# TensorE's first stage as two loops, and two edge-table compares on GpSimd, in a graph-attention layer

## The chip, the cores and the metric

The kernel runs on one core of one Trainium2 chip. The metric is the device time of one execution in microseconds; the kernel before took 474.52 us (median of 3 runs, 474.12 to 474.85). TensorE does the matmuls, VectorE (DVE) and ScalarE (ACT) read PSUM and split numbers, GpSimd (POOL) issues scattered transfers and does small arithmetic, SyncE (SP) issues most transfers.

## The reference

One layer over 384 nodes of 1024 features, in float32:

```
xn = layernorm(x)                                        # 384 x 1024
q, k, v = xn @ wq.T + bq, xn @ wk.T + bk, xn @ wv.T + bv
q2, k2, v2 = heads(q @ wiq.T + biq), heads(k @ wik.T + bik), heads(v @ wiv.T + biv)   # 16 heads of 64
mask = full((384, 384), -inf); mask[src, dst] = softplus(w)[type - 1]   # 12288 edges; diagonal: w[3] where empty
attn = softmax(q2 @ k2^T / 8 + mask)
gnn  = (attn @ v2) @ wo.T + bo
mq, mk = exp(-(xn @ Wq + bq)^2 / 2), exp(-(xn @ Wk + bk)^2 / 2)
mix  = (sum_per_head(mq * mk) * (xn @ Wv + bv)) @ Wo + bo
x    = x + gnn + mix
h    = layernorm(x)      # then the expert with the smallest loss is chosen for all of h
out  = x + h @ base_W.T + base_b + (relu(h @ down_W[e] + down_b[e]) @ up_W[e] + up_b[e]) @ conv_W[e].T + conv_b[e]
```

## The kernel before

Every float32 matrix product is made of three products of a shorter format: each operand is split into a high part (rounded by ScalarE, w_hi or T_hi) and a low part (the rest, by VectorE, w_lo or T_lo), and TensorE adds hi x hi, lo x hi and hi x lo into one PSUM bank.

The engines' programs are written out by hand, one instruction stream for each, and nothing but semaphores ties them together. Weights come as blocks of 128x1024 (512 KB) in rotating slots: SyncE loads a block into raw, ScalarE makes w_hi (line 536), VectorE w_lo (line 895), TensorE uses both and frees them.

The first stage has 32 jobs, 8 for each of q, k, v and q2. A job (column_job, lines 1272 to 1284) waits for the slot's high part (hi_ready), issues 16 matmuls of 128x384 (line 1278), waits for the low part (lo_ready), issues 8 more (line 1283) and frees the slot (w_used). Ahead of it TensorE waits until the PSUM bank is free (bank_free). Jobs go round four slots and four banks, so job a has slot and bank a % 4 and use number a // 4. Slot 3 of the four lies in the memory of other tiles, so its blocks are called mask, probT_hi and probT_lo in the profile. Jobs 0 and 1 are written out apart; jobs 2 to 31 come from one Python loop, which leaves 30 x 24 matmuls one behind the other in TensorE's program. Jobs 2 to 23 multiply xT, jobs 24 to 31 T0.

Beside it, the edge mask is built. GpSimd scatters the 12288 edge values into four tables in device memory (96 indirect transfers, line 454), since an edge may occur twice and the last one counts; then it loads them back (line 463): table 0 into mask, tables 1 to 3 into the tile U. VectorE fills the diagonal (lines 975 and 979) and merges tables 1 to 3 into mask, one after another (merge_table): a compare with the blank value -1e30 writes present (line 986), and a predicated copy takes what is present (line 988). present is one place in U, so each compare waits for the copy before it. Behind the merge come the eight head pairs: scores (line 1404), softmax (maximum at 1060, exponential on ScalarE at 659, reciprocal at 1069), turning by a transfer through device memory, and the product with V (line 1416). GpSimd's next work behind the table loads is a cast of V (line 485).

Of the kernel before, what the change touches and what calls it, by code (L numbers as in the profile page):

```python
# [18 lines left out]
U32 = mybir.dt.uint32  # L19
ALU = mybir.AluOpType  # L20
# [5 lines left out]
N = 384  # L26
D = 1024
NT = N // P
KB = D // P
# [3 lines left out]
CH = E // P  # L33
CJ = 3
STEPS = CH // CJ
STREAMS = 4
# [7 lines left out]
ABSENT = -1e30  # L44
# [5 lines left out]
FIRST = 32  # L50
# [4 lines left out]
A_SLOTS = (0, 1, 2, SLOTS + SPARE - 1)  # L55
A_USES = [(A_SLOTS[a % 4], a // 4) for a in range(FIRST)]
A_BANKS = (0, 1, 6, 7)
# [43 lines left out]
def gps_layer(nc, x, out, weights, conv, down, upT, up_b, down_b, conv_b, disc, bias_cols,  # L101
              rows, edge_weights, edge_rows, edge_cols, consts):
    with ExitStack() as ctx:
        def sb(name, shape, dt):
            return ctx.enter_context(nc.sbuf_tensor(name, shape, dt))

        def sem(name):
            return ctx.enter_context(nc.semaphore(name))
# [10 lines left out]
        xT = [sb(f"xT_{c}", [P, KB, N], F32R) for c in ("hi", "lo")]  # L119
        T0 = [sb(f"T0_{c}", [P, KB, N], F32R) for c in ("hi", "lo")]  # L120
# [6 lines left out]
        U = sb("U", [P, 6 * D], F32)  # L127
# [2 lines left out]
        key_row = U[:, 3456:3456 + 2 * CJ * P].rearrange("p (s n) -> p s n", s=2)  # L130
        key_junk = U[:, 4224:4352]
        later = [U[:, g * NT * N:(g + 1) * NT * N].rearrange("p (t n) -> p t n", t=NT) for g in range(STREAMS - 1)]
        present = U[:, 4608:4608 + NT * N].rearrange("p (t n) -> p t n", t=NT)
        prob = U[:, 0:2 * NT * N].rearrange("p (h t n) -> p h t n", h=2, t=NT)
        sq_q = U[:, 2304:2688]
        sq_k = U[:, 2688:3072]
# [105 lines left out]
        bank_free = [sem(f"bank_free{s}") for s in range(len(A_BANKS))]  # L242
        dup_ready = sem("dup_ready")
# [3 lines left out]
        diag_step = sem("diag_step")  # L247
        scattered = [sem(f"scattered{g}") for g in range(STREAMS)]
        table_in = [sem(f"table_in{g}") for g in range(1, STREAMS)]
        mask_step = sem("mask_step")  # L250
        v_copied = sem("v_copied")
        v_tile = sem("v_tile")
        vh_ready = sem("vh_ready")
# [169 lines left out]
        def _(pool):  # L423
# [25 lines left out]
            for k in range(CH):  # L449

                g = QUARTERS[k % STREAMS]
# [6 lines left out]
            for g, into in enumerate([mask[:]] + later):  # L458
                pool.wait_ge(scattered[g], 16 * (DEEP + 1))
                if g == 0:  # L460

                    pool.wait_ge(lo_ready[A_SLOTS[3]], FIRST // 4 + 1)
                pool.dma_start(into, tables[g].rearrange("(t p n) o -> p t (n o)", t=NT, p=P)).then_inc(
                    table_in[g - 1] if g else first_mask_in, 16)

            def mix_lo(j):

                pool.wait_ge(mh_ready, j + 1)
                pool.tensor_tensor(T2[1][:, j, :], mix_v, T2[0][:, j, :].bitcast(F32),  # L469
                                   ALU.subtract).then_inc(ml_ready, 1)  # L470
# [339 lines left out]
        def _(dve):  # L810
# [36 lines left out]
            def turned(t, which=0):  # L847
                b = LN_BANKS[which][t]
                return PS[:, b:b + 2, :].rearrange("p b (k n) -> p (b k) n", k=4), slice(t * P, (t + 1) * P)
# [48 lines left out]
            for t in range(NT):  # L898
                dve.wait_ge(xt_hi, t + 1)
                src, r = turned(t)  # L900
# [81 lines left out]

            def merge_table(g):

                dve.wait_ge(table_in[g], 16)
                dve.tensor_scalar(present, later[g], ABSENT, None, ALU.not_equal).then_inc(mask_step, 1)
                dve.wait_ge(mask_step, 2 * g + 1)
                dve.copy_predicated(mask[:].rearrange("p t n -> p (t n)"),
                                    present.bitcast(U32).rearrange("p t n -> p (t n)"),
                                    later[g].rearrange("p t n -> p (t n)")).then_inc(mask_step, 1)  # L990
                dve.wait_ge(mask_step, 2 * g + 2)

            for a in range(FIRST):
                job(a)
# [33 lines left out]
            for g in range(STREAMS - 1):  # L1028
                merge_table(g)
# [232 lines left out]
        def _(pe):  # L1262
# [9 lines left out]
            def column_job(slot, use, src, bank):  # L1272

                o = PS[:, bank, 0:N]
                pe.wait_ge(hi_ready[slot], use + 1)
                for part in range(2):
                    for k in range(KB):
                        pe.matmul(o, w_hi[slot][:, k * P:(k + 1) * P], src[part][:, k, :],  # L1278
                                  start=(k == 0 and part == 0), stop=False)
                pe.wait_ge(lo_ready[slot], use + 2)  # L1280
                for k in range(KB):
                    wl = w_lo[slot][:, k * P:(k + 1) * P]
                    last = pe.matmul(o, wl, src[0][:, k, :], start=False, stop=(k == KB - 1))  # L1283
                last.then_inc(w_used[slot], 1)
# [58 lines left out]
            def whole_part(a, wide, part, start, stop):  # L1343

                for k in range(KB):
                    last = pe.matmul(PS[:, A_BANKS[a], 0:N], wide[A_SLOTS[a]][:, k * P:(k + 1) * P],  # L1346
                                     xT[part][:, k, :], start=(start and k == 0), stop=(stop and k == KB - 1))
                return last
# [16 lines left out]
            whole_part(1, w_hi, 1, False, False)  # L1365
            pe.wait_ge(lo_ready[A_SLOTS[1]], 2)
            whole_part(1, w_lo, 0, False, True).then_inc(w_used[A_SLOTS[1]], 1)
            for a in range(2, FIRST):
                pe.wait_ge(bank_free[a % 4], a // 4 + 1)
                column_job(*A_USES[a], T0 if a >= 3 * KB else xT, A_BANKS[a % 4])  # L1370

            for half in range(2):
                for kp in range(4):
# [238 lines left out]
```

## Time and profile before

| | us |
|---|---|
| median of 3 runs (lowest, highest) | 474.52 (474.12, 474.85) |
| the profiled execution's own time | 474.66 |
| its span, first to last instruction | 472.9 |
| TensorE busy | 465.9 |
| VectorE, ScalarE, GpSimd busy | 342.3, 262.2, 157.2 |

The span is what the profile's rows cover; its own time is 1.8 us longer. TensorE's matmuls are pipelined: one 128x384 matmul is shown with 0.33 us, but the next begins 0.17 us behind it. So a dense stretch is read from the distance of the starts, not from the durations.

### The profile page before, as it was taken

The numbers are of one execution on the slowest core, as the hardware profiler recorded it, in microseconds if no ns is written. First come the engines' busy times: TensorE is split into PE (matmuls) and PEld (weight loads), VectorE is DVE, ScalarE is ACT, GpSimd is POOL, SyncE is SP. The second block draws the span as 40 slices with busy tenths as digits, with TensorE's granted clock in tenths as the row PEclk, the third lists the DMA queues.
The fourth block names the chain that finished last, engine by engine and source line by source line (L and its number), as shares of the span: only waits on it lengthen the run. The fifth ranks groups of instructions, "written<-read, shape, count | busy, mean of one in ns | idle before, by whom it ended". The sixth has DMA issues, their size and how long they took to land.

```text
span 472.9 us, 7361 instructions
## 1 busy us (share of the span) xinstructions
PE 465.9 (99%) x2533; PEld 432.4 (91%) x2533; DVE 342.3 (72%) x796; ACT 262.2 (55%) x429; POOL 157.2 (33%) x176
## 2 busy tenths in 40 slices
PE   7999999999999999999999999999999999999996
PEld 5999999999999888999999999999998888888885
DVE  6979966677626259687978888796966794587294
ACT  3734433333324245788989889897974542163170
POOL 3147677777767741002130202212142000050200
PEclk9999999999999999999999999999999999999999
DMA  8877756655444454577675766766679835210463
GB/s 243 325 230 230 239 195 167 176 182 180 154 152 153 133 200 179 175 226 253 205 232 184 235 192 197 247 180 224 192 240 382 308 115 179 89 46 0 155 247 133
DMA packets 39049, 91.92 MB, mean 194 GB/s; under 512 B 7410, under 2 KB 20306, under 8 KB 38884
## 3 DMA queue, kind: packets, MB, share of 16 engines
q1 hardware_dynamic: 33604, 83.15, 54.0%
q0 software_dynamic: 4832, 7.45, 4.7%
q10 hardware_dynamic: 576, 0.85, 0.5%
q8 instruction: 20, 0.33, 0.3%
q14 instruction: 17, 0.14, 0.1%
HBM read 77.96 MB, written 13.47 MB: 193 GB/s over the span
## 4 chain that ended last, share of the span: by engine, by line
PE 87%; DVE 5%; DMA 3%; ACT 3%; issue 1%; SPq 0%; DVEq 0%; ACTq 0%
PE PS L1278 32%; PE PS L1288 28%; PE PS L1283 16%; PE PS L1416 3%; PE PS L1404 2%; DMA turn<-U 2%; PE PS L1535 2%; PE PS L1346 2%; DMA U<-x 1%; DVE U L1076 1%; DVE w_lo L895 1%; PE PS L1266 1%; ACT U L659 1%; PE PS L1539 1%; ACT w_hi L536 1%
## 5 line engine op out<-in xcount | busy, mean ns | idle before, releaser
L895 DVE TENSOR_TENSOR w_lo<-raw,w_hi 128x1024 fp32r<-128x1024 f32 x86 | 104.4, 1225 | 45.0 <-ACT w_hi L536 45.0
L536 ACT ACTIVATE w_hi<-raw 128x1024 fp32r<-128x1024 f32 x87 | 90.8, 1054 | 68.5 <-PE PS L1288 44.1
L454 POOL DMA_INDIRECT table<-evalue,where x96 | 103.0, 1073 | 45.7 <-issue 25.2
L1283 PE MATMUL PS<-xT_hi,w_lo 128*128 128x384 f32 x320 | 61.9, 334 | 0.0
L1278 PE MATMUL PS<-xT_hi,w_hi 128*128 128x384 f32 x320 | 61.9, 334 | 0.0
L1278 PE MATMUL PS<-xT_lo,w_hi 128*128 128x384 f32 x320 | 61.9, 334 | 0.0
L1278 PEld LDWEIGHTS PS<-xT_lo,w_hi 128*128 128x128 f32 x320 | 56.0, 188 | 0.0
L1278 PEld LDWEIGHTS PS<-xT_hi,w_hi 128*128 128x128 f32 x320 | 56.0, 188 | 0.0
L1283 PEld LDWEIGHTS PS<-xT_hi,w_lo 128*128 128x128 f32 x320 | 56.0, 188 | 0.0
L469 POOL TENSOR_TENSOR T_lo<-U,T_hi 128x384 fp32r<-128x384 f32 x8 | 8.2, 1020 | 97.8 <-ACT T_hi L733 97.8
L1288 PE MATMUL PS<-w_hi,T_hi 128*128 128x512 f32 x144 | 40.0, 391 | 0.0
L1288 PE MATMUL PS<-w_hi,T_lo 128*128 128x512 f32 x144 | 39.8, 389 | 0.0
L950 DVE SCALAR_TENSOR_TENSOR U<-U,V,cst 128x128 f32<-128x128 f32 x96 | 33.6, 350 | 6.0 <-DMA U<-key_dram 3.7
L1288 PE MATMUL PS<-w_lo,T_hi 128*128 128x512 f32 x144 | 37.8, 389 | 0.0
L598 ACT ACTIVATE T_hi<-PS,bias 128x384 fp32r<-128x384 f32 x24 | 13.8, 576 | 41.7 <-PE PS L1283 41.7
L1288 PEld LDWEIGHTS PS<-w_hi,T_lo 128*128 128x128 f32 x144 | 27.0, 188 | 5.7
L1288 PEld LDWEIGHTS PS<-w_lo,T_hi 128*128 128x128 f32 x144 | 27.0, 188 | 5.6
L1288 PEld LDWEIGHTS PS<-w_hi,T_hi 128*128 128x128 f32 x144 | 27.0, 188 | 5.2
L1076 DVE STREAM_TRANSPOSE U<-U 128x384 f32<-128x384 f32 x48 | 24.0, 551 | 10.5 <-DMA turn<-U 10.5
L659 ACT ACTIVATE U<-U,nmax 128x384 f32<-128x384 f32 x48 | 28.9, 605 | 3.7 <-DVE nmax L1064 3.7
L965 DVE SCALAR_TENSOR_TENSOR T_lo<-PS,bias,T_hi 128x384 fp32r<-128x384 f32 x24 | 14.8, 615 | 16.1 <-ACT T_hi L598 16.1
L666 ACT ACTIVATE U<-U,rsum 128x384 f32<-128x384 f32 x48 | 25.8, 604 | 0.0
(241 smaller groups left out, 817.1 us busy)
## 6 DMA issues: line engine op xcount, KB each, us to landing
raw<-weights SPq DMA_DIRECT2D x84, 512.0 KB, 4.6
turn<-U SPq DMA_DIRECT2D x16, 576.0 KB, 4.0
U<-turn SPq DMA_DIRECT2D x64, 144.0 KB, 2.9
U<-key_dram SPq DMA_DIRECT2D x32, 192.0 KB, 4.1
mask<-weights SPq DMA_DIRECT2D x9, 512.0 KB, 5.1
table<-Q POOLq DMA_DIRECT2D x4, 576.0 KB, 9.5
V<-conv SPq DMA_DIRECT2D x4, 512.0 KB, 5.4
U<-table POOLq DMA_DIRECT2D x3, 576.0 KB, 7.5
```

Of the source, the lines that this page charges most:

```text
L454: pool.indirect_dma_start(tables[g], bass.IndirectOffsetOnAxis(ap=where[:, k:k + 1], axis=0), evalue[:, k:k + 1], None, bounds_check=N * N ...
L536: act.activation(w_hi[slot][:], raw[slot][:], ACT.Copy).then_inc(hi_ready[slot], 1)
L659: act.activation(prob[:, h, t, :], prob[:, h, t, :], ACT.Exp, bias=nmax[:, h, t:t + 1], scale=SCALE, accum_out=ssum[:, h, t:t + 1]).then_i ...
L666: act.activation(prob[:, h, t, :], prob[:, h, t, :], ACT.Copy, scale=rsum[:, h, t:t + 1]).then_inc(prob_ready, 1)
L895: dve.tensor_tensor(w_lo[slot][:], raw[slot][:], w_hi[slot][:].bitcast(F32), ALU.subtract).then_inc(lo_ready[slot], 1)
L950: dve.scalar_tensor_tensor(out=key_junk, in0=key_row[:, s, c * P:(c + 1) * P], scalar=ekey[:, ch0 + c:ch0 + c + 1], in1=tri, op0=ALU.is_eq ...
L965: dve.scalar_tensor_tensor(out=dst[1][:, j, :], in0=PS[:, A_BANKS[a % 4], 0:N], scalar=bias[:, a:a + 1], in1=dst[0][:, j, :].bitcast(F32), ...
L1076: dve.transpose(blocks.rearrange("p (c m t i) -> p t m c i", c=NQ, m=NT, t=NT)[:, t], prob[:, h, t, :].rearrange("p (m c i) -> p m c i", m ...
L1278: pe.matmul(o, w_hi[slot][:, k * P:(k + 1) * P], src[part][:, k, :], start=(k == 0 and part == 0), stop=False)
L1283: last = pe.matmul(o, wl, src[0][:, k, :], start=False, stop=(k == KB - 1))
L1288: return pe.matmul(bank, src[part][:, 2 * kp + k2, t * P:(t + 1) * P], weights_in[slot][:, k2 * HALF:(k2 + 1) * HALF], start=start, stop=stop)
L1416: last = pe.matmul(PS[:, 7, 0:N], vs[:, m, h, :], probT[part][:, m, :], start=(m == 0 and part == 0), stop=(m == NT - 1 and part == 1))
```

## The change

TensorE: jobs 2 and 3 stay written out. Jobs 4 to 31 become two loops that run on TensorE alone, each pass four jobs (one for each slot and bank): five passes over xT, two over T0. The numbers that the jobs wait for come from the loop's register. GpSimd: behind its four table loads it compares tables 1 and 2 with the blank value (is_gt instead of not_equal) and raises found. present has two places now, the first where the key rows of the duplicate search were, the second where it was; so the first compare waits for that search (dup_ready) and the second for the diagonal (diag_step). VectorE keeps the compare of table 3 and the three copies.

```diff
--- before.py
+++ after.py
@@ -130,7 +130,7 @@
         key_row = U[:, 3456:3456 + 2 * CJ * P].rearrange("p (s n) -> p s n", s=2)
         key_junk = U[:, 4224:4352]
         later = [U[:, g * NT * N:(g + 1) * NT * N].rearrange("p (t n) -> p t n", t=NT) for g in range(STREAMS - 1)]
-        present = U[:, 4608:4608 + NT * N].rearrange("p (t n) -> p t n", t=NT)
+        present = [U[:, c:c + NT * N].rearrange("p (t n) -> p t n", t=NT) for c in (3456, 4608)]
         prob = U[:, 0:2 * NT * N].rearrange("p (h t n) -> p h t n", h=2, t=NT)
         sq_q = U[:, 2304:2688]
         sq_k = U[:, 2688:3072]
@@ -248,6 +248,7 @@
         scattered = [sem(f"scattered{g}") for g in range(STREAMS)]
         table_in = [sem(f"table_in{g}") for g in range(1, STREAMS)]
         mask_step = sem("mask_step")
+        found = sem("found")
         v_copied = sem("v_copied")
         v_tile = sem("v_tile")
         vh_ready = sem("vh_ready")
@@ -463,6 +464,15 @@
                 pool.dma_start(into, tables[g].rearrange("(t p n) o -> p t (n o)", t=NT, p=P)).then_inc(
                     table_in[g - 1] if g else first_mask_in, 16)
 
+            for g in range(STREAMS - 2):
+
+                pool.wait_ge(table_in[g], 16)
+                if g == 0:
+                    pool.wait_ge(dup_ready, CH)
+                if g == 1:
+                    pool.wait_ge(diag_step, 2 * NT)
+                pool.tensor_scalar(present[g], later[g], ABSENT, None, ALU.is_gt).then_inc(found, 1)
+
             def mix_lo(j):
 
                 pool.wait_ge(mh_ready, j + 1)
@@ -982,13 +992,16 @@
 
             def merge_table(g):
 
-                dve.wait_ge(table_in[g], 16)
-                dve.tensor_scalar(present, later[g], ABSENT, None, ALU.not_equal).then_inc(mask_step, 1)
-                dve.wait_ge(mask_step, 2 * g + 1)
+                if g < STREAMS - 2:
+                    dve.wait_ge(found, g + 1)
+                else:
+                    dve.wait_ge(table_in[g], 16)
+                    dve.tensor_scalar(present[0], later[g], ABSENT, None, ALU.not_equal).then_inc(found, 1)
+                    dve.wait_ge(found, g + 1)
                 dve.copy_predicated(mask[:].rearrange("p t n -> p (t n)"),
-                                    present.bitcast(U32).rearrange("p t n -> p (t n)"),
+                                    present[g % 2].bitcast(U32).rearrange("p t n -> p (t n)"),
                                     later[g].rearrange("p t n -> p (t n)")).then_inc(mask_step, 1)
-                dve.wait_ge(mask_step, 2 * g + 2)
+                dve.wait_ge(mask_step, g + 1)
 
             for a in range(FIRST):
                 job(a)
@@ -1365,9 +1378,15 @@
             whole_part(1, w_hi, 1, False, False)
             pe.wait_ge(lo_ready[A_SLOTS[1]], 2)
             whole_part(1, w_lo, 0, False, True).then_inc(w_used[A_SLOTS[1]], 1)
-            for a in range(2, FIRST):
-                pe.wait_ge(bank_free[a % 4], a // 4 + 1)
-                column_job(*A_USES[a], T0 if a >= 3 * KB else xT, A_BANKS[a % 4])
+            for a in (2, 3):
+                pe.wait_ge(bank_free[a], 1)
+                column_job(*A_USES[a], xT, A_BANKS[a])
+
+            for src, begin, end in ((xT, 1, 3 * KB // 4), (T0, 3 * KB // 4, FIRST // 4)):
+                with pe.Fori(0, end - begin) as i:
+                    for s in range(4):
+                        pe.wait_ge(bank_free[s], i + (begin + 1))
+                        column_job(A_SLOTS[s], i + begin, src, A_BANKS[s])
 
             for half in range(2):
                 for kp in range(4):
```

TensorE's program around the start of job 4, before (names as in the profile; x8 is eight alike):

```order
L1278 MATMUL PS<-xT_lo,probT_hi 128x384 x8
L1283 MATMUL PS<-xT_hi,probT_lo 128x384 [waits lo_ready6]
L1283 MATMUL PS<-xT_hi,probT_lo 128x384 x7
L1278 MATMUL PS<-xT_hi,w_hi 128x384 [waits hi_ready0,bank_free0]
L1278 MATMUL PS<-xT_hi,w_hi 128x384 x7
L1278 MATMUL PS<-xT_lo,w_hi 128x384 x8
```

And now, at the same place (column_job's lines are 1291 to 1296 there, the loops' line is 1386):

```order
L1291 MATMUL PS<-xT_lo,probT_hi 128x384 x8
L1296 MATMUL PS<-xT_hi,probT_lo 128x384 [waits lo_ready6]
L1296 MATMUL PS<-xT_hi,probT_lo 128x384 x7
L1386 UNCONDITIONAL_BRANCH
L1386 ISA
L1291 MATMUL PS<-xT_hi,w_hi 128x384 [waits hi_ready0,bank_free0]
L1291 MATMUL PS<-xT_hi,w_hi 128x384 x7
L1291 MATMUL PS<-xT_lo,w_hi 128x384 x8
L1293 REGISTER_ALU
```

Up to the branch TensorE issues 21 + 8 + 4 + 16 + 104 = 153 matmuls and transposes in both. The end of a pass, which before was simply the next job:

```order
L1296 MATMUL PS<-xT_hi,probT_lo 128x384 x7
L1386 REGISTER_ALU
L1386 COMPARE_AND_BRANCH
L1386 UNCONDITIONAL_BRANCH
L1386 ISA
L1291 MATMUL PS<-T_hi,w_hi 128x384 [waits hi_ready0,bank_free0]
```

The last four rows are the way into the second loop; the branch back goes to the first ISA row. VectorE's program at the merge, before:

```order
L986 TENSOR_SCALAR U<-U 128x1152 [waits table_in1]
L988 COPY_PREDICATED mask<-U 128x1152 [waits mask_step]
L986 TENSOR_SCALAR U<-U 128x1152 [waits table_in2,mask_step]
L988 COPY_PREDICATED mask<-U 128x1152 [waits mask_step]
L986 TENSOR_SCALAR U<-U 128x1152 [waits table_in3,mask_step]
L988 COPY_PREDICATED mask<-U 128x1152 [waits mask_step]
```

and now:

```order
L1001 COPY_PREDICATED mask<-U 128x1152 [waits found]
L1001 COPY_PREDICATED mask<-U 128x1152 [waits found,mask_step]
L999 TENSOR_SCALAR U<-U 128x1152 [waits table_in3,mask_step]
L1001 COPY_PREDICATED mask<-U 128x1152 [waits found]
```

Two of three compares have left VectorE. GpSimd has them, now:

```order
L464 DMA U<-table 128x3x384 [waits scattered3]
L474 ISA
L474 TENSOR_SCALAR U<-U 128x1152 [waits dup_ready,table_in1]
L474 TENSOR_SCALAR U<-U 128x1152 [waits diag_step,table_in2]
L495 CAST vs<-V 128x6x64 [waits v_copied]
```

The two compares stand between the last table load and the cast of V, which before followed each other. The ISA row stood behind the cast before.

## Rows read from the trace of the kernel before

**Rows 1.** The page: span, busy time, TensorE's granted clock, the chain that ended last.

```profile
span 472.9 us, 7361 instructions
PE 465.9 (99%) x2533; PEld 432.4 (91%) x2533; DVE 342.3 (72%) x796; ACT 262.2 (55%) x429; POOL 157.2 (33%) x176
...
PEclk9999999999999999999999999999999999999999
...
PE 87%; DVE 5%; DMA 3%; ACT 3%; issue 1%; SPq 0%; DVEq 0%; ACTq 0%
```

**Rows 2.** The waits of TensorE: us in total, times, longest.

```profile
PE PS L1416 <- DVE probT_lo L1041: 0.2, 1, 0.2
```

**Rows 3.** In order of time, 29 to 50 us: start us, us, engine, line.

```profile
29.80 1.34 PEld L1283 LDWEIGHTS PS<-xT_hi,probT_lo 128*128 128x128 f32 x8 [0.26 <-DVE probT_lo L895]
31.30 1.55 PE L1278 MATMUL PS<-xT_hi,w_hi 128*128 128x384 f32 x8
31.45 1.22 DVE L895 TENSOR_TENSOR w_lo<-raw,w_hi 128x1024 fp32r<-128x1024 f32 x1
47.94 1.55 PE L1278 MATMUL PS<-xT_hi,w_hi 128*128 128x384 f32 x8
```

**Rows 4.** In order of time, VectorE, 177 to 190 us.

```profile
177.95 1.23 DVE L895 TENSOR_TENSOR w_lo<-raw,w_hi 128x1024 fp32r<-128x1024 f32 x1 [0.83 <-ACT w_hi L536]
179.09 0.75 DVE L986 TENSOR_SCALAR U<-U 128x1152 f32<-128x1152 f32 x1
...
184.64 1.55 DVE L988 COPY_PREDICATED mask<-U 128x1152 f32<-128x1152 uint32 x1
...
187.80 0.17 DVE L1064 TENSOR_SCALAR nmax<-smax 128x3 f32<-128x3 f32 x1
...
189.54 2.35 DVE L895 TENSOR_TENSOR w_lo<-raw,w_hi 128x1024 fp32r<-128x1024 f32 x2
```

**Rows 5.** The chain of waits, 189 to 206 us: start us, us, what.

```profile
189.10 3.72 ACT U L659 x12
...
192.84 0.18 DVE rsum L1069
...
205.95 1.33 PE PS L1416 x6
```

**Rows 6.** In order of time, TensorE, the first scores, 184 to 187 us.

```profile
184.78 0.45 PE L1404 MATMUL PS<-T_hi,q_hi 64*128 64x384 f32 x2
...
186.56 1.66 PE L1278 MATMUL PS<-T_hi,w_hi 128*128 128x384 f32 x8
```

**Rows 7.** The page, DMA queues: packets, MB, share of 16 engines.

```profile
q8 instruction: 20, 0.33, 0.3%
```

**Rows 8.** The same queue in 41.5 to 42.5 us.

```profile
q8 instruction: 1, 0.02, 5.5%
```

**Rows 9.** TensorE by stretch: us, busy (matmuls), clock, DMA share, GB/s.

```profile
0.00:42.00 42.00, 39.09 (x215) 1.00 0.81 263
```

**Rows 10.** DMA issues: times, KB each, median us to landing.

```profile
U<-down_b SPq DMA_DIRECT2D x1, 0.2 KB, 2.4
```

**Rows 11.** In order of time, GpSimd, the whole span.

```profile
2.75 1.08 POOL L438 MEMSET Q<- 128x1152 f32 x1
...
185.55 0.96 POOL L485 CAST vs<-V 128x384 fp32r<-128x384 f32 x1 [11.74 <-ACT V L613]
...
220.97 0.50 POOL L485 CAST vs<-V 128x384 fp32r<-128x384 f32 x1 [2.54 <-PE PS L1416]
221.55 1.01 POOL L487 TENSOR_TENSOR vs<-V,vs 128x384 fp32r<-128x384 f32 x1
```

**Rows 12.** Line 463: its table loads into U; landing of the first and the last.

```profile
L463 POOL DMA_DIRECT2D U<-table x3: 758/774/812, 171.5 to 173.1; - x3
...
DMA to landing us min/median/max: 6.8/6.8/6.8
...
DMA to landing us min/median/max: 10.1/10.1/10.1
```

## The prediction

> **What bounds the kernel now.** I read the page's shares first: TensorE is busy 99% of a span of 472.9 us and carries 87% of the chain that ended last, at full granted clock (the 2.4 GHz level) from end to end [rows 1]. So only what makes TensorE wait, or stops it waiting, can move the end. The list of waits says how little it waits: between its start-up and its tail the one row is 0.2 us at line 1416 [rows 2]. The stretch that the loops replace is the densest of all. In the order of time each group of eight 384-column matmuls takes 1.39 us (31.30 to 47.94 is exactly twelve of them: 16.64 us, four jobs), and job 4, the first that goes into a loop, begins at 31.30 [rows 3]. Nothing can be won inside it; a loop can only cost.
>
> The edge tables matter elsewhere, on VectorE between 179 and 187 us, where three compares (0.75 us each) and three predicated copies (1.55 us each) stand ahead of the first softmax [rows 4]. The chain of waits shows what carries the program there: not VectorE's merge but ScalarE, which copies the last tile of V, splits two weight blocks, loads its table and starts the exponentials at 189.10; VectorE comes in at 192.84, and the first value product starts at 205.95 [rows 5]. That is where the 0.2 us of [rows 2] are. A microsecond added to this chain is a microsecond at the end, since TensorE is already waiting for it.
>
> **The change, part by part: the loops.** The matmuls are the same 28 x 24; what comes on top is control. One pass of a loop holds 96 matmuls, one fused register instruction, two register additions and a compare-and-branch; a plain branch leads into each loop, and the jobs' waits compare with a register. The profile before has no row for a register or branch instruction of TensorE. Two rows bound them. The 18 narrow score matmuls from 184.78 to 186.56 are 36 instructions (a weight load and a matmul each) in 1.78 us [rows 6], so TensorE's sequencer hands over an instruction in 0.05 us or less, while a wide pair is used up in 0.173 us. From below the price is nothing; from above I take 0.3 us for each, near the one stretch without work that the weight loads show in this stage, 0.26 us [rows 3].
>
> These are paid beside the matmuls as long as the sequencer is ahead of the array. How far ahead it is can be read from code loading. The instruction queue q8 brought 20 pieces, 0.33 MB, so 16 KB each [rows 7]. For 2533 matmuls that is one piece per 127, so the second border lies near matmul 250. A piece came between 41.5 and 42.5 [rows 8], but by 42.0 only 215 matmuls had started [rows 9]. If this is the second one, called for as the sequencer passes the second border, it is some 32 matmuls ahead, 32 x 0.173 = 5.5 us. Two places need a look.
> - Entry into the first loop. Job 3's low part was 0.26 us late (weight load at 29.80, released by VectorE) [rows 3], so here the lead is near nothing. The 16 instructions behind it are handed over in at most 0.8 us, by 30.6, and the next weight load is due at about 31.1. Three control instructions stand between (a branch, the register instruction, a wait), and they have 0.5 us; at 0.3 us each they would be 0.4 us late. I take 0, by the nearer row, and keep 0.4 as the end.
> - The back edges: four taken ones in the first loop, one in the second. The first pass ends with matmul 153 + 96 = 249 (153 from the order of the instructions), that is, right at the second border, so the loop's head and its tail lie in different pieces of code. If the head has to be brought again, the price is at least a small transfer's 2.4 us from issue to landing [rows 10], with 1.1 us for the piece itself (0.3% of 16 x 472.9 us, over 20) [rows 7]: about 3.5 us. The queue in front of the array holds 5.5 us. And the next job's weights are not late: VectorE's split for job 4 began at 31.45, ended at 32.7 and was used at about 34.1 [rows 3], and that margin grows, since a job takes TensorE 4.16 us and VectorE's share of it less. After a fetch of 3.5 us the sequencer is 2 us ahead and gains about 0.1 us with every matmul. I take 0 for each edge.
>
> The Trainium skill (Runtime: NRT & Kernel Launch, Instruction fetch mechanics) says that a taken branch whose target is not in the current two pages forces a fetch before execution can go on, and calls it a stall. That rule speaks against this change, and it is the first rival below; what I set against it is only the 5.5 us of queued matmuls.
>
> **The compares.** VectorE loses two compares (2 x 0.79 us with their gap) and gains two waits for GpSimd. GpSimd gains two compares of 128x1152. It has no such row: the 128x1152 memset took 1.08 us, the cast of 128x384 0.50 us (three times that is 1.5), the tensor_tensor of 128x384 1.01 us (three times 3.05) [rows 11]. A compare reads one operand like the cast, so I take 1.3 us and keep 1.08 and 3.05 as ends. The start is set by the tables: the first of the three lands at 171.5 + 6.8 = 178.3, the last at 173.1 + 10.1 = 183.2 [rows 12].
>
> Do GpSimd and VectorE work side by side there? The cast at 185.55 took 0.96 us beside a predicated copy that ran until 186.19, against 0.50 us alone [rows 4, 11]: GpSimd stood still until VectorE was done. So I add them up one after another. Compare 0 can run once the weight split of 177.95 is over, 179.1 to 180.4; then copy 0 (1.55), compare 1 (1.3), copy 1 (1.55) in either order to 184.8; then compare 2 on VectorE, 0.76, and copy 2, 1.55: 187.2 with the gaps. Before it was 186.19 [rows 4]. The merge ends 1.0 us later, not 1.6 us earlier. If copies and compares overlapped, the last table (183.2) would set it, and it would end at about 185.6. The Trainium skill (SBUF — State Buffer, SBUF: two separate sides) calls the shared port pair an exclusive lock that blocks the loser; the trace agrees for the cast.
>
> What waits for the merge: the first maximum, which before was ready 1.78 us after it at 187.97 [rows 4] and now at 189.0; ScalarE begins its exponentials at 189.10 [rows 5]. Cost nothing. Behind the maxima VectorE has two weight splits of 2.35 us together, begun at 189.54 [rows 4], now at 190.6, ending at 192.9, and the second reciprocal, which stood at 192.84 [rows 5], comes at 193.1. That is 0.2 us on the chain. GpSimd's next work, the cast for V at 185.55, is not delayed, and nobody else queues behind its two waits. If the compares cost 1.08 us and nothing blocks, the merge ends at 185.5 and the chain gains nothing, because ScalarE holds it. The other end is the second rival.
>
> Sum: loops 0, compares +0.2 us. The profiled execution took 474.66 us (span 472.9 and 1.8 around it), so 474.9; it was 0.14 above the median of the three runs, 474.52. I say 474.8.
>
> **The rivals.** (1) The back edge stalls. If the border is crossed and the sequencer first lets the piece after the border arrive and only then fetches the head, it is two transfers: 2 x 3.5 = 7 us, less the 5.5 us of queue, 1.5 us at each of four edges: +6 us, 480.7; with one slow transfer of 6.5 us, +4 us, 478.7. What speaks for it: the border lies in the last job, and the DMA engines are 81% busy in the first 42 us [rows 9]. Against it: 20 borders were crossed before without a single wait of TensorE. This is the slower one: it decides as soon as a fetch takes longer than 5.5 us.
> (2) The compares cost like a two-operand operation, 3.05 us. Then the merge ends at 179.1 + 3.05 + 1.55 + 3.05 + 1.55 + 2.35 = 190.7; the maximum comes at 192.4, the exponentials 3.3 us late, the second reciprocal some 3.7 us: 478.4. At 2.2 us for a compare the merge ends at 189.0, the maximum comes 1.7 us after 189.1, and the end is some 1.9 us later, 476.6. The point from which it costs is near 1.3 us, so it is close; for it the first use of an operation on GpSimd, against it that only one operand is read.
> (3) Faster: the two engines overlap after all, VectorE's earlier splits pull the chain, and the wait of 0.2 us at 205.95 goes [rows 2]: 474.66 - 0.2 = 474.5. More than that TensorE does not wait anywhere in reach, so this one can't be told from no change.
>
> **How the numbers follow.** Forecast 0.70, rival 1 0.13, rival 2 0.12, rival 3 0.05. A measurement of this kernel tells about 0.2% from no change, 0.95 us. Of the forecast I give 0.03 to slower and 0.07 to faster, for what no row of before shows; of rivals 1 and 2 0.02 and 0.01 are too small to see, and all of rival 3. Slower 0.03 + 0.11 + 0.11 = 0.25; faster 0.07; the same 0.60 + 0.02 + 0.01 + 0.05 = 0.68. The forecast's own range is 474.1 to 475.6. For 8 in 10 I go up into both slow cases until a tenth is left above: 473.9 to 477.8.
>
> **What would show it.** In the profile after: the eights of the first stage still 1.39 us apart with no idle before them, at the end of each pass of twelve in particular (47.9, 64.6, 81.2, 97.9), and job 31 ending near 147.8. A gap at just those times is rival 1. The number of q8 pieces: 16 or 17 if a loop keeps its code, some four to eight more if the head is fetched again. On GpSimd the two compares, 1.1 to 1.5 us each, not lying over VectorE's copies; VectorE's third copy ending at about 187; the exponentials at 189.1 after the start of the stage as before; the first value product at most 0.3 us later. Wrong I am if TensorE waits over 1 us in all between 31 and 206 us, or if its matmuls are not spaced as before within a pass.

## The result, and the profile after

The changed kernel took 482.55 us (median of 4 runs: 483.10, 482.61, 482.49, 480.51); the kernel before took 474.33 beside it. The medians lie 8.2 us apart, and the time is outside the range given. The ratio is 1.0143 (95% interval 1.0094 to 1.0191), which is 4.5 to 9.1 us: slower. Here and in the table below a ratio is estimated from the faster runs of each kernel alone (those within 1.5% of its fastest) and is not the quotient of the medians beside it. The profiled execution took 483.1 us, its span is 481.3, against 472.9. All rows here are of one kernel each; in the changed kernel the numbers of VectorE's lines are 10 to 13 higher and those of TensorE's 13 to 19 (1278 is now 1291, 1060 is 1073).

The page of the changed kernel, to be laid beside [rows 1, 7]:

```profile
span 481.3 us, 7393 instructions
PE 469.3 (98%) x2533; PEld 435.5 (90%) x2533; DVE 341.5 (71%) x794; ACT 261.5 (54%) x429; POOL 167.7 (35%) x178
...
PEclk9999999999999999799999999999999999999999
...
q8 instruction: 16, 0.26, 0.2%
...
PE 72%; DMA 11%; issue 5%; DVE 5%; POOL 4%; ACT 1%; POOLq 0%; DVEq 0%; SPq 0%; ACTq 0%
```

GpSimd's busy time grew by 10.5 us. In the chain that ended last transfers now have 11% (3% before) and GpSimd 4% (none before), and one slice of 40, from 192 to 205 us, has less than the full clock. The list of TensorE's waits shows what is new against [rows 2]:

```profile
PE PS L1291 <- DVE smax L1073: 5.2, 1, 5.2
```

**The first stage.** In order of time (start, duration, engine, line), the last part of job 3, the start of the first loop, of its second pass and of the second loop, and the first matmul behind the stage:

```profile
30.45 1.34 PEld L1296 LDWEIGHTS PS<-xT_hi,probT_lo 128*128 128x128 f32 x8 [0.88 <-DVE probT_lo L905]
...
31.95 1.55 PE L1291 MATMUL PS<-xT_hi,w_hi 128*128 128x384 f32 x8
...
48.59 1.55 PE L1291 MATMUL PS<-xT_hi,w_hi 128*128 128x384 f32 x8
...
115.15 1.55 PE L1291 MATMUL PS<-T_hi,w_hi 128*128 128x384 f32 x8
...
148.43 1.55 PE L1301 MATMUL PS<-w_hi,T_hi 128*128 128x512 f32 x6
```

From 31.95 to 48.59 are the same 16.64 us as in [rows 3], and five passes to 115.15 are 5 x 16.64. The 28 jobs in the loops take 116.48 us (31.95 to 148.43), and they took 116.48 before (31.30 to 147.78). Neither the control instructions nor the back edges cost anything. Nor was code fetched for them: the queue q8 brings one piece between 42 and 43 us and then none until 128, where the kernel before has one each near 63, 84, 105 and 126 us. So at no back edge of the first loop was the head brought again. The whole stage is 0.65 us late because job 3's low part came 0.88 us late instead of 0.26 [rows 3], ahead of the loops.

**The merge.** GpSimd and VectorE of the changed kernel, 172 to 197 us, beside [rows 4]:

```profile
172.97 0.82 POOL L464 DMA_DIRECT2D mask<-table  x1 [3.47 <-DMA table<-evalue,where]
...
179.97 8.67 POOL L474 TENSOR_SCALAR U<-U 128x1152 f32<-128x1152 f32 x2 [3.86 <-DMA U<-table]
...
189.29 2.16 POOL L497 TENSOR_TENSOR vs<-V,vs 128x384 fp32r<-128x384 f32 x1
```

```profile
179.88 1.23 DVE L905 TENSOR_TENSOR w_lo<-raw,w_hi 128x1024 fp32r<-128x1024 f32 x1
184.14 1.55 DVE L1001 COPY_PREDICATED mask<-U 128x1152 f32<-128x1152 uint32 x1 [3.03 <-POOL U L474]
188.74 1.88 DVE L1001 COPY_PREDICATED mask<-U 128x1152 f32<-128x1152 uint32 x1 [3.05 <-POOL U L474]
190.65 1.42 DVE L999 TENSOR_SCALAR U<-U 128x1152 f32<-128x1152 f32 x1
192.10 1.43 DVE L1001 COPY_PREDICATED mask<-U 128x1152 f32<-128x1152 uint32 x1
193.58 0.55 DVE L1073 CUSTOM_DVE_ANT_0 U<-PS,mask 128x384 f32<-128x384 f32 x1
...
196.68 0.08 DVE L1073 DVE_READ_ACCUMULATOR2_ANT smax<- 128x1 f32 x1
```

The chain of waits splits the 8.67 us into the two compares, and takes the way over both:

```profile
179.97 4.14 POOL U L474
184.10 0.08 issue
184.18 4.46 POOL U L474
```

Two compares that VectorE did in 0.75 us each take GpSimd 4.14 and 4.46 us. VectorE stands for 3.03 and 3.05 us, and the merge ends at 193.5 instead of 186.2: 7.3 us later. Of these, 0.9 are the later start of the first compare, which waited for its table (179.97 for 179.09), 3.4 the first compare, 2.5 the step from the first copy to the third compare (184.14 to 190.65, before 179.88 to 183.85), and 0.5 the last compare and copy, beside which GpSimd works on V. Not all of the 7.3 comes from the compares. The mask's table was late too, so VectorE's diagonal and the split behind it ended at 181.1 instead of 179.2. With its three compares still on VectorE, this merge would have ended 1.9 us later than before (an estimate from these rows), and 5.4 us are left for the move.

**TensorE.** Its waits and matmuls behind the scores, and the clock by stretch (us, busy, granted clock, DMA share, GB/s):

```profile
190.09 1.55 PE L1296 MATMUL PS<-T_hi,w_lo 128*128 128x384 f32 x8
196.82 2.93 PE L1291 MATMUL PS<-xT_hi,w_hi 128*128 128x384 f32 x8 [5.17 <-DVE smax L1073]
199.55 2.76 PE L1291 MATMUL PS<-xT_lo,w_hi 128*128 128x384 f32 x8
202.11 1.59 PE L1296 MATMUL PS<-xT_hi,w_lo 128*128 128x384 f32 x8
203.54 1.55 PE L1291 MATMUL PS<-xT_hi,w_hi 128*128 128x384 f32 x8
```

```profile
190.00:195.00 5.00, 1.65 (x10) 1.00 0.00 0
195.00:200.00 5.00, 3.18 (x10) 0.54 0.18 53
200.00:205.00 5.00, 5.00 (x25) 0.78 0.74 272
205.00:210.00 5.00, 5.00 (x31) 1.00 0.48 127
```

Here is what I had not seen. In the code of the first pair, TensorE itself waits for VectorE's sixth score read (score_read, whose count starts at 1, so the 7 waited for is six reads) between the pair's first and second column job. Before, the sixth read ended at 189.43 and the second job began at 190.82, as it was due: 1.4 us of slack. Now the job was due at 191.5 and the read ends at 196.76. Behind the wait the granted clock is 0.54 of full, near the lower level (1.2 GHz), and three groups of eight (196.82 to 203.54) take 6.72 us instead of 4.16. So 0.65 + 5.17 + 2.56 = 8.4 us, and the span is 8.4 us longer. By the starts alone, the group behind these three begins 8.55 us later (203.54 for 194.99), so the sum closes to about 0.2 us.

### The profile page after: what moved, and what is told of

It is laid out like the page before. It is cut to its first block, busy times and chain, and to the rows that moved or that the text cites. A ratio compares the mean times of both kernels' runs of the same rounds, so it can differ in the third digit from the quotient of the medians.

```text
span 481.3 us, 7393 instructions
## 1 busy us (share of the span) xinstructions
PE 469.3 (98%) x2533; PEld 435.5 (90%) x2533; DVE 341.5 (71%) x794; ACT 261.5 (54%) x429; POOL 167.7 (35%) x178
## 4 chain that ended last, share of the span: by engine, by line
PE 72%; DMA 11%; issue 5%; DVE 5%; POOL 4%; ACT 1%; POOLq 0%; DVEq 0%; SPq 0%; ACTq 0%
PE PS L1291 28%; PE PS L1301 20%; PE PS L1296 14%; DMA table<-evalue,where 5%; PE PS L1435 3%; PE PS L1423 2%; POOL table L455 2%; POOL U L474 2%; PE PS L1554 2%; DMA mask<-table 1%; DMA turn<-U 1%; DVE w_lo L905 1%; DMA raw<-weights 1%; DMA U<-x 1%; DMA key_dram<-V 1%
## 5 line engine op out<-in xcount | busy, mean ns | idle before, releaser
L1291 PE MATMUL PS<-xT_hi,w_hi 128*128 128x384 f32 x320 | 63.3, 339 | 5.2 <-DVE smax L1073 5.2
L1291 PE MATMUL PS<-xT_lo,w_hi 128*128 128x384 f32 x320 | 63.1, 339 | 0.0
L1291 PEld LDWEIGHTS PS<-xT_hi,w_hi 128*128 128x128 f32 x320 | 57.1, 191 | 5.5 <-DVE smax L1073 5.5
L1291 PEld LDWEIGHTS PS<-xT_lo,w_hi 128*128 128x128 f32 x320 | 57.2, 191 | 0.0
```

## The experiments

The kernels ran in five sessions, each with the kernel before beside them. In the first three the kernel before had medians of 497 to 500 us instead of 474, though one of its runs took 480.37. The trace of loops_2 shows a part of it: in 90 to 120 us the transfers moved 135 GB/s and TensorE was busy for 27.0 us of the 30, where the kernel before in its own profile had 173 GB/s and 30.0 us. The gaps of TensorE (10.8 us in the whole trace) are put down to nothing that the profile shows, so their cause is open. These sessions say little of small differences in time, but their traces do tell durations and waits. I draw nothing from the ratios of session 1: the 29 runs of the kernel before reach from 487 to 507 us, and the other medians lie within 0.1% of theirs but for e5_fill, although the ratios of both e1_loops and e2_compares lie above 1 by more than their intervals. The fourth and fifth were like the first measurement; I call those undisturbed and the first three disturbed.

| session; the kernel before | run | median us | ratio (95%) |
|---|---|---|---|
| 1; 497.38 | e1_loops, loops alone | 497.70 | 1.0125 (1.002, 1.0229) |
| 1 | e2_compares, compares alone | 497.80 | 1.0106 (1.0051, 1.0162) |
| 1 | e3_add | 497.81 | 1.0032 (0.9987, 1.0078) |
| 1 | e5_fill | 502.99 | 1.0129 (1.0077, 1.018) |
| 2; 498.10 | loops_alone | 500.23 | none |
| 2 | compares_alone | 496.35 | none |
| 2 | late_merge | 505.73 | none |
| 2 | prices | 503.14 | one run |
| 3; 500.00 | loops_2 | 503.19 | 1.0066 (0.9982, 1.015) |
| 3 | compares_2 | 500.63 | 1.004 (0.9978, 1.0102) |
| 3 | late_merge_2 | 509.96 | 1.0285 (1.0142, 1.0427) |
| 3 | one_compare | 498.06 | 0.9991 (0.9934, 1.0048) |
| 4; 475.15 | late_tables | 482.82 | 1.0155 (1.0094, 1.0215) |
| 4 | late_tables_one | 484.62 | 1.0193 (1.0133, 1.0252) |
| 4 | late_tables_compares | 489.44 | 1.0298 (1.0223, 1.0374) |
| 4 | late_tables_fill | 490.69 | 1.0308 (1.0248, 1.0367) |
| 5; 476.47 | compares_3 | 480.77 | 1.0114 (1.007, 1.0158) |
| 5 | loops_3 | 476.36 | 1.0012 (0.9982, 1.0042) |

### Each edit alone

loops_3 has TensorE's loops, and GpSimd and VectorE as before; compares_3 has the compares, and TensorE's jobs 2 to 31 written out. The same two kernels ran as e1_loops, loops_alone and loops_2, and as e2_compares, compares_alone and compares_2; none of those six traces has a wait for a score read.

Expected of compares_3:

> The two compares on GpSimd alone, where the kernel before takes 475 us in its runs again. Theory: TensorE waits 4.5 to 5.5 us for the seventh score read, and the time is 5.5 to 8.5 us over the kernel before. Rival (the loops carry a part, by the later start of job 3's low parts and the later tables): no more than 5 us over it.

Expected of loops_3:

> The loops alone, on the same terms. Theory: no wait for a score read, and within 1 us of the kernel before. Rival (the loops put the first stage and the tables late): 0.65 us at job 3, tables over 2 us later, and 1 to 3 us over the kernel before.

The loops alone make no difference that can be told: 1.0012, so between 0.9 us faster and 2.0 us slower. The compares alone cost 1.0114, 5.4 us (3.3 to 7.5), a little under the 5.5 to 8.5 expected, as is the wait (4.01 us for 4.5 to 5.5). The rival's bound, 5 us, lies inside the interval, so the times alone do not exclude that the loops carry a part. In the trace of compares_3 everything of the changed kernel is there, in somewhat smaller size:

```profile
178.98 8.64 POOL L474 TENSOR_SCALAR U<-U 128x1152 f32<-128x1152 f32 x2 [4.57 <-DMA U<-table]
```

```profile
195.91 2.93 PE L1291 MATMUL PS<-xT_hi,w_hi 128*128 128x384 f32 x8 [4.01 <-DVE smax L1073]
198.63 1.76 PE L1291 MATMUL PS<-xT_lo,w_hi 128*128 128x384 f32 x8
200.23 1.55 PE L1296 MATMUL PS<-xT_hi,w_lo 128*128 128x384 f32 x8
```

It has the late low part of job 3 as well (0.6 us), without any loop; so that does not come from the loops. Its merge ends 0.9 us before that of the changed kernel (192.63 for 193.53), as its diagonal was ready 1.1 us earlier, and with the shorter wait TensorE lost 1.5 us behind it and not 2.6. loops_3 shows, against my expectation, what late tables do by themselves, with a wait of its own in a kernel that moved no compare:

```profile
172.76 0.80 POOL L463 DMA_DIRECT2D mask<-table  x1 [1.79 <-DMA table<-evalue,where]
```

```profile
193.10 1.68 PE L1278 MATMUL PS<-xT_hi,w_hi 128*128 128x384 f32 x8 [1.26 <-DVE smax L1060]
194.62 1.55 PE L1278 MATMUL PS<-xT_lo,w_hi 128*128 128x384 f32 x8
```

GpSimd issued the first table load at 170.70 in the profile before, at 172.97 in the changed kernel, 172.76 in loops_3 and 171.27 in compares_3; in the four kernels of session 4, none with loops, at 170.89 to 172.55. The scattered transfers ahead of it end up to 2.3 us apart from one execution to the next, and the 1.4 us of slack do not cover that. The execution in this trace took 478.32 us, 2.0 more than the median of loops_3, so most of its runs pay less. Of the three signs that its rival named two came, the wait at job 3 and tables 2 us later; the third, 1 to 3 us more time, did not. Whether the loops add to the tables' lateness is not settled: both traces with loops in undisturbed sessions lie high, one of six without them lies as high.

### The price of the compare

prices is the kernel before with eight operations on GpSimd in its idle time at 20 us, each waited for. It ran once:

```diff
+            price(pool.tensor_scalar(into, wide, ABSENT, None, ALU.is_gt))
...
+            price(pool.tensor_copy(into, wide))
+            price(pool.tensor_tensor(into, wide, wide, ALU.subtract))
```

> The kernel before, with eight operations on GpSimd in its idle time ahead of the gathers of the first stage, each waited for: compare, maximum, add and multiply with a constant on 128 x 1152, compare and add on 128 x 384, a copy and a subtraction of two tiles on 128 x 1152. Theory (an ordinary price of GpSimd's operations with a constant): the four wide ones take 3.1 us alike, the narrow ones 1.0 to 1.1. Rival (the compare is dear by its kind): compare over 3 us, add and multiply under 1.5 us. The copy: 1.5 us by the 384-wide one of the kernel before (0.50); the subtraction 3 us by the 384-wide one (1.01).

```profile
20.17 3.17 POOL L457 TENSOR_SCALAR Q<-Q 128x1152 f32<-128x1152 f32 x1
...
26.63 3.19 POOL L459 TENSOR_SCALAR Q<-Q 128x1152 f32<-128x1152 f32 x1
29.91 3.13 POOL L460 TENSOR_SCALAR Q<-Q 128x1152 f32<-128x1152 f32 x1
33.12 1.17 POOL L461 TENSOR_SCALAR Q<-Q 128x384 f32<-128x384 f32 x1
...
36.38 1.21 POOL L463 COPY Q<-Q 128x1152 f32<-128x1152 f32 x1
37.67 3.04 POOL L464 TENSOR_TENSOR Q<-Q 128x1152 f32<-128x1152 f32 x1
```

Compare, add and multiply cost the same, 3.13 to 3.19 us, and as much as an operation on two tiles (3.04); a copy costs 1.21. VectorE was not idle beside them, and it was the one held up: an operation on 128x4 that began 0.06 us behind the first compare took 2.90 us, against 0.16 in the kernel before. The narrow add began 0.3 us behind a split of VectorE and took 1.95 us instead of the narrow compare's 1.17. (This kernel's own time is no measure: ScalarE was made to wait for the eight.) e3_add is the changed kernel with the two GpSimd compares replaced by an add of 1e30; its adds took 3.42 and 3.13 us. Its time decides nothing, since no score read was waited for in its trace.

> The changed kernel, but GpSimd finds what is present by adding 1e30 (a blank becomes 0, anything else stays non-zero) instead of comparing. If it is the comparison that is dear on GpSimd (4.1 us where a cast of this size would be 1.5), the adds take about 1.3 to 1.5 us each and the time falls to 474.5 us. If every tensor_scalar of 1152 columns costs 4 us there, nothing changes: 482 us.

The rival that the compare is dear by its kind falls. The Trainium skill (GPSIMD Engine Reference, Performance versus the Vector engine) gives tensor_tensor, by its two inputs, about 2.6 cycles for each element, and a tight loop at best about 1.8; by these an operation with a constant could be the cheaper one. Here it is not.

3.13 us is the price alone. In the changed kernel the first compare began 0.09 us behind VectorE's split (1.23 us, two operands) and took 4.14, about 1.0 more; the second shared its time with a predicated copy of 1.55 us and took 4.46, 1.3 more. Where no VectorE operation lay beside it, in late_tables_one below, the first compare took 3.15 us. That is the blocking that the cast showed [rows 11].

### Where the tables come in time

Expected of compares_alone:

> The two compares on GpSimd alone; TensorE's first stage is written out as before. Theory: GpSimd takes 3 to 4.5 us for each, TensorE waits for the seventh score read of the first pair, and the time is that of the changed kernel, 480.5 to 483 us (ratio 1.013 to 1.018). Rival (the loss is shared with the loops): 476 to 480 us.

It failed, and that told most. TensorE's first stage ended 22 us later there than in the changed kernel (170.62 for 148.43), VectorE had the diagonal ready 19 us later, but the first table was there only 5.5 us later:

```profile
185.49 3.15 POOL L474 TENSOR_SCALAR U<-U 128x1152 f32<-128x1152 f32 x1 [4.87 <-DMA U<-table]
199.37 3.13 POOL L474 TENSOR_SCALAR U<-U 128x1152 f32<-128x1152 f32 x1 [10.73 <-DVE mask L989]
```

```profile
200.79 2.54 DVE L905 TENSOR_TENSOR w_lo<-raw,w_hi 128x1024 fp32r<-128x1024 f32 x1 [1.58 <-ACT w_hi L546]
203.26 3.11 DVE L1001 COPY_PREDICATED mask<-U 128x1152 f32<-128x1152 uint32 x2
```

The first compare is done 10.7 us before VectorE has the diagonal ready, the second lies beside VectorE's split, and TensorE does not wait for a score read at all. Even then little is won: the split takes 2.54 us instead of 1.23, since GpSimd holds it up, so 1.3 of the 1.6 us that VectorE was spared are gone. compares_2 and one_compare (the changed kernel with only the first compare on GpSimd) had no wait either, and no difference in time that can be told (up to 1.0% and 0.5% slower is possible). Expected of one_compare:

> The changed kernel with only the first of the two compares on GpSimd; the second and third on VectorE. Theory: the first copy starts near 184.1 us as in the changed kernel, the rest takes 0.8 + 1.55 + 0.8 + 1.55 us, and the merge ends near 188.9 us, 2.7 us later than before. Of that 1.2 to 1.5 us are slack, so TensorE waits 0.5 to 1.5 us for the seventh score read: 475.0 to 477 us where the kernel before takes 474.3. Rival (each compare moved costs its share of the loss, half of 8.2 us): 478.4 us.

Neither side of it was tested, since the wait was hidden.

### A late merge with no compare moved

late_merge is the kernel before with eight more compares on VectorE ahead of the merge and nothing new on GpSimd:

```diff
+                if g == 0:
+                    for n in range(8):
+                        dve.tensor_scalar(present, later[g], ABSENT, None, ALU.not_equal).then_inc(extra, 1)
+                        dve.wait_ge(extra, n + 1)
```

> The kernel before, with eight more compares of the first later table on VectorE (0.76 us and a wait each, about 6.4 us) and nothing on GpSimd. Theory (a late merge is what costs, whoever is late): the merge ends near 192.5 us, TensorE waits 4.5 to 5 us for the seventh score read, and the time is 479 us, up to 481.5 where the granted clock falls behind the wait. Rival (what costs is the contention of VectorE and GpSimd at the port they share, or the work behind the compares on GpSimd): no more than the 0.2 us for each us that the path over ScalarE was given in the prediction, so under 476 us.

```profile
218.52 2.93 PE L1283 MATMUL PS<-xT_hi,w_hi 128*128 128x384 f32 x8 [5.58 <-DVE smax L1065]
221.24 2.16 PE L1283 MATMUL PS<-xT_lo,w_hi 128*128 128x384 f32 x8
```

The wait is 5.58 us, in late_merge_2 too, where TensorE loses 2.5 us behind it. That is the changed kernel's wait and clock, with no compare on GpSimd, so a late merge is enough for both, and contention is only one way to get one. In time late_merge_2 was to be 4.5 to 7.5 us over the kernel before; its ratio is 1.0285, 14 us. It rests on two runs in a disturbed session (interval 7 to 21 us), so it speaks against the rival's "under 2 us" and no more; that the cost is the same as in the changed kernel was not shown.

### The loss with tables held back

In session 4 I held the three later tables back by 16 memsets of 128 x 512 on GpSimd (9.3 us) behind the mask's load, with no, one or both compares on GpSimd.

```diff
+                if g == 0:
+                    for n in range(16):
+                        pool.memset(spend[:], 0.0).then_inc(spent, 1)
+                        pool.wait_ge(spent, n + 1)
```

> The kernel before, with 16 memsets of 128 x 512 on GpSimd between the load of the mask table and those of the three later tables (0.5 us each, 8 to 9 us). They put the landing of the tables back to where VectorE comes to them, as it was in the profile of the kernel before (table in about 0.8 us ahead). Theory (cover): the merge takes 7.2 us from the landing or from VectorE's arrival, whichever is later, and TensorE waits 0 to 2 us for the seventh score read. Time within 2 us of the kernel before of the same call.

> The same memsets, and the two compares on GpSimd. Theory: with the tables late the compares have no cover: the first takes 3.1 to 4.1 us, the second 4.4 us beside the copy, and the merge takes 12 to 12.5 us instead of 7.2. TensorE's wait for the seventh score read is 4 to 5.5 us longer than with the same memsets and the compares on VectorE; behind it the granted clock is near half, and eights take up to 2.7 us instead of 1.39. Time 4 to 8 us over the other one. Rival (the compares cost nothing in themselves; their run alone showed no loss): the two take the same time within the scatter of 3 us, with waits within 1 us of each other.

> The same memsets, and only the first compare on GpSimd. Theory (threshold): the merge takes 3.1 to 4.1 + 1.55 + 0.8 + 1.55 + 0.8 + 1.55 = 9.4 to 10.4 us, so the wait is 2.2 to 3.2 us longer than with none moved, and 2 to 3 us shorter than with both. Rival (the loss comes from the second compare alone, which stands behind the diagonal's mask): as with none moved.

TensorE was in time in session 4, so the memsets put the tables 7 us too late for VectorE, and late_tables by itself is 7.7 us slower than the kernel before; that expectation failed. The comparison among the three holds. Their waits, with none, one and both compares moved:

```profile
197.05 2.93 PE L1284 MATMUL PS<-xT_hi,w_hi 128*128 128x384 f32 x8 [5.49 <-DVE smax L1066]
```

```profile
200.20 2.93 PE L1297 MATMUL PS<-xT_hi,w_hi 128*128 128x384 f32 x8 [8.31 <-DVE smax L1079]
```

```profile
202.53 2.93 PE L1297 MATMUL PS<-xT_hi,w_hi 128*128 128x384 f32 x8 [10.52 <-DVE smax L1079]
```

From the start of the first compare to the end of the merge it is 7.8 us (185.92 to 193.76), 10.1 (186.83 to 196.91) and 12.4 us (186.82 to 199.25). The first compare moved adds 2.2 us, the second 2.3, and the waits grow by 2.8 and 2.2 (the tables came 0.9 us later in the second trace and the third than in the first). The spans of these traces are 480.6, 482.9 and 486.4 us, to which the clock's part (below) adds unequally. The medians are 482.82, 484.62 and 489.44. So the loss is not the second compare's alone. Without slack a later merge is a longer wait: the merge ends 3.15 and then 2.34 us later, and TensorE waits 2.8 and 2.2 us more.

### The clock behind the wait

The time that the three eights behind the wait took, less the 4.16 us that they take at full clock:

| trace | wait us | lost behind it us |
|---|---|---|
| loops_3 | 1.26 | 0.1 |
| compares_3 | 4.01 | 1.5 |
| changed kernel | 5.17 | 2.6 |
| late_tables | 5.49 | 2.3 |
| late_merge_2 | 5.58 | 2.5 |
| late_tables_one | 8.31 | 1.5 |
| late_tables_compares | 10.52 | 2.6 |

The loss is there in every trace with a wait of 4 us or more, it is between 1.5 and 2.6 us, and it does not grow with the wait. The clock falls before the work comes back, as late_merge shows (us, busy, granted clock, DMA share, GB/s; the wait ends at 218.52):

```profile
214.00:218.00 4.00, 0.00 (x0) 0.71 0.00 0
218.00:222.00 4.00, 3.48 (x11) 0.50 0.29 86
```

In late_tables_compares the whole of 197 to 202 us stands at 0.50, and TensorE does nothing in it. The runs without a trace agree: three of the changed kernel's four have a mean granted clock of 0.993 and took 482.5 to 483.1 us, the fourth has 0.999, as the kernel before, and took 480.51.

To test that standing idle is the cause, late_tables_fill keeps TensorE busy ahead of the wait:

```diff
+                    if j == 0:
+                        for n in range(22):
+                            pe.matmul(PS[:, 7, :], xT[0][:, n % KB, 0:P],
+                                      xT[0][:].rearrange("p k n -> p (k n)")[:, 0:HALF], start=True, stop=True)
```

> The same memsets and both compares on GpSimd, and 22 matmuls of 512 columns into bank 7, whose result nobody reads, ahead of TensorE's wait for the seventh score read (0.22 us each, 4.8 us). Theory (the clock falls because TensorE stands idle): the granted clock stays 1.00 behind the wait, the next eights take 1.39 us each, and the time is 1 to 2.6 us under that of the same kernel without the fill where the wait is 4.5 us or more. Rival (the fall has another cause): the eights still take up to 2.7 us, and the time is the same or longer.

```profile
193.03 5.19 PE L1468 MATMUL PS<-xT_hi 128*128 128x512 f32 x22
203.55 2.93 PE L1297 MATMUL PS<-xT_hi,w_hi 128*128 128x384 f32 x8 [5.34 <-DVE smax L1079]
206.28 2.51 PE L1297 MATMUL PS<-xT_lo,w_hi 128*128 128x384 f32 x8
```

It missed. I took 22 matmuls for a wait of 5 us, but the wait to be filled was 10.5 us, so 5.34 us of standing were left, and 2.3 us were lost behind them as elsewhere; the time is not better (490.69, 489.44 without). e5_fill is the changed kernel with the same fill in session 1; it found no wait to fill, and its 5 us more (502.99) are near the fill's own length.

> The changed kernel with 22 matmuls of 512 columns of no use, written to a PSUM bank that nobody reads, between the first and the second column job of the first head pair, where TensorE waited 5.2 us. They last 22 x 0.227 = 5.0 us, so they fit in the wait. If the clock fell because TensorE stood still, the granted clock stays 1.00 and the time falls by the 2.6 us that the slow stretch cost: 480.0 us. If the slow stretch had another cause, 482.5 us or more.

The table and the stretches show that the clock falls while TensorE stands in a wait of this length; that a filled wait would avoid the loss was not shown.

## Why the prediction was wrong

- **The loops: right.** The eights stayed 1.39 us apart, no gap at the ends of passes, 16 pieces of code instead of 20, and loops_3 is within the scatter. The first rival, a stall at the back edge with 4 to 6 us, did not come. But what I set against it, a queue of 5.5 us that hides a fetch, was not put to the test: no piece of code came between 43 and 128 us, so no fetch was forced. The Trainium skill's rule on branches (Runtime: NRT & Kernel Launch, Instruction fetch mechanics) is for a target outside the two pages held; the trace fits a head that was still held, and what a longer loop would cost is open.
- **The price of a compare: the step that failed.** "A compare reads one operand like the cast, so I take 1.3 us and keep 1.08 and 3.05 as ends." It is 3.13 alone, just above the upper end, and 4.14 and 4.46 in place. By that the merge ends 7.3 us later, of which 5.4 are the move's, and not the 1.0 us that I summed. I had two rows for operations on float32 tiles, a cast and an operation with two tiles, and chose by the number of operands. An operation with a constant belonged to the arithmetic, not to the copies.
- **The lock: right in kind, half applied.** I added copies and compares one behind the other, but let the first compare begin when the split was over, where in the run it lay beside it, and left the last compare and copy free of GpSimd, whose work on V now falls there (1.42 us for a compare that took 0.76). "The cast for V ... is not delayed" was wrong as well: it began at 188.70, 3.1 us later, but TensorE did not wait for V.
- **The second rival had the mechanism and was 4 us short.** It ended the merge at 190.7; it was 193.5. The missing 2.9 us: table 0.9, first compare 1.1, the copy behind the second 0.4, the last pair 0.5. It then led the lateness to the end over ScalarE's exponentials, 478.4.
- **What bounds: a wait that I didn't list.** "What waits for the merge: the first maximum" was incomplete. TensorE's own wait for the sixth read had 1.4 us of slack, so every us of merge beyond that holds it up directly. This did not make the forecast fail: at my own merge, 1.0 us later, that wait costs nothing. It had the path wrong for the case that came. A list of waits shows only waits that were paid; this one stood in the code with its slack uncounted. And I had no term for the clock, 2.6 us of the 8.4.
- **The chances.** Slower had 0.25, and the second rival 0.12 though its price was the nearest row for arithmetic. Its point of decision was 1.3 us, exactly my own value; a forecast that sits on the point where the cost begins is not worth 0.70.

## What to carry to other kernels

Before moving work to another engine, find or make a row for that very kind of operation on it, and let arithmetic be priced by arithmetic. For everything that ends later, go through all who wait for it in the code, and note for each the slack (when it was due, less when the thing was ready); the smallest slack decides, and a wait of TensorE of 4 us or more cost 1.5 to 2.6 us on top here, by its clock. Work on an engine that starts only when a transfer lands is free or dear by who comes first there, so look at it in more than one trace.

## What the runs showed of the hardware

- GpSimd, float32, 128x1152: operation with a constant 3.13 us (compare, add or multiply alike), two tiles 3.04, copy 1.21, memset 1.08 [rows 11]; VectorE does the compare in 0.75 [rows 4].
- The blocking goes both ways: GpSimd's compare took 4.46 us beside a copy of VectorE, and VectorE's split 2.54 us instead of 1.23 beside a compare of GpSimd. A small one is held as long: one on 128x4 took 2.90 us instead of 0.16.
- A TensorE loop with 96 matmuls (192 instructions with their weight loads) in a pass ran five passes without a gap of the array and with no piece of code fetched behind its first pass (16 pieces in the whole kernel for 20).
- Behind waits of 4.0 to 10.5 us TensorE lost 1.5 to 2.6 us at a granted clock near 0.5, the lower of its two levels; the clock had fallen while it stood. Behind 1.3 us it stayed at full clock.
